# Bias of the edge list written by ScalarE, upper halves copied by Pool, edge stages in a new order

## The reference, cut to what matters

```python
hi = x @ W1[:H];  hj = x @ W1[H:]
h = relu(hi[:, :, None, :] + hj[:, None, :, :] + b1)   # one vector for each pair i, j
y = layernorm(h @ W2 + b2) * gamma + beta              # over the features
out = einsum('bij,bijh->bih', adj, y)                  # sum over the edges of node i
x = layernorm(x + out)
```

## Time and profile before

| what | value |
|---|---|
| three runs | 448.45, 449.18, 449.66 us |
| the profiled execution: its own time | 449.61 us |
| its span in the trace | 447.9 us |
| PE busy | 429.5 us (96%), 3391 instructions |
| DVE busy | 422.7 us (94%), 1555 |
| ACT busy | 393.8 us (88%), 1001 |
| Pool busy | 353.6 us (79%), 651 |

### The profile page before, as it was taken

How to read it: one execution, slowest core, us unless ns; L and a number is a source line. 1 busy time by engine, 2 the same in 40 slices (tenths; PEclk the granted TensorE clock), 3 DMA queues, 4 the chain that set the end, 5 groups by cost and what they waited for, 6 DMA issues and landing times. The chain is left out here.

```text
span 447.9 us, 14059 instructions
## 1 busy us (share of the span) xinstructions
PE 429.5 (96%) x3391; PEld 403.8 (90%) x3391; DVE 422.7 (94%) x1555; ACT 393.8 (88%) x1001; POOL 353.6 (79%) x651
## 2 busy tenths in 40 slices
PE   7599989999999999999999999999999999999993
PEld 3599989999999999898999999999999999999992
DVE  6999999999999999998999999999999999999976
ACT  2378979999999899979899999999999999999994
POOL 3569979999999899953776878787878787878772
PEclk9989999999999999999999999999999999999998
DMA  6134334445444743232422223222323232323111
GB/s 225 43 86 124 101 127 159 154 157 159 155 157 152 240 162 120 80 129 78 136 89 73 88 66 92 66 92 64 94 64 94 64 94 63 95 65 97 59 37 50
DMA packets 50939, 47.60 MB, mean 106 GB/s; under 512 B 5584, under 2 KB 42576, under 8 KB 50896
## 3 DMA queue, kind: packets, MB, share of 16 engines
q1 hardware_dynamic: 49760, 46.45, 33.7%
q10 hardware_dynamic: 1136, 0.66, 0.5%
HBM read 28.22 MB, written 18.87 MB: 105 GB/s over the span
## 5 line engine op out<-in xcount | busy, mean ns | idle before, releaser
L1621 PE MATMUL bank<-w2c,hE 128*128 128x128 f32 x512 | 68.3, 277 | 0.4 <-ACT bank L928 0.4
L1621 PEld LDWEIGHTS bank<-w2c,hE 128*128 128x128 f32 x512 | 63.5, 192 | 2.6 <-issue 0.7
L1289 DVE TENSOR_TENSOR ym<-bank,wE 128x512 f32<-128x512 f32 x64 | 43.4, 684 | 4.3 <-POOL wE L775 3.3
L1264 DVE TENSOR_REDUCE ssum<-sqE 128x4 f32<-128x512 f32 x63 | 42.7, 678 | 3.0 <-ACT sqE L945 2.7
L1122 DVE BATCH_NORM_STATS2 stats<-t 128x6 f32<-128x128 f32 x192 | 44.5, 273 | 1.0 <-issue 1.0
L945 ACT ACTIVATE sqE<-bank 128x512 f32<-128x512 f32 x63 | 38.0, 603 | 8.0 <-PE bank L1621 8.0
L915 ACT ACTIVATE hE<-bank,front 128x512 f32<-128x512 f32 x64 | 43.5, 680 | 1.5 <-PE bank L1601 1.5
L742 POOL TENSOR_TENSOR half<-ym 128x512 f32<-128x512 f32 x31 | 39.6, 1276 | 5.7 <-DVE ym L1289 2.1
L775 POOL TENSOR_TENSOR wE<-erstd,fits 128x12 f32<-128x12 f32 x31 | 6.6, 213 | 44.8 <-DVE erstd L1278 44.8
L726 POOL TENSOR_TENSOR gHl<-gH,gHu 128x512 fp32r<-128x512 f32 x32 | 40.8, 1276 | 1.2 <-ACT gHu L899 1.2
L928 ACT ACTIVATE bank<-b2c 128x512 f32<-128x512 f32 x62 | 37.4, 604 | 0.5 <-DVE ym L1289 0.4
(11 more groups left out here) (192 smaller groups left out, 1643.6 us busy)
## 6 DMA issues: line engine op xcount, KB each, us to landing
hh_scratch<-hh SPq DMA_DIRECT2D x32, 256.0 KB, 2.2
gH<-hh_scratch SPq DMA_DIRECT2D x32, 256.0 KB, 2.7
A<-adj_groups SPq DMA_DIRECT2D x32, 128.0 KB, 2.1
res_scratch<-res SPq DMA_DIRECT2D x32, 128.0 KB, 2.0
gRES<-res_scratch SPq DMA_DIRECT2D x32, 128.0 KB, 2.0
AT<-adjT_groups SPq DMA_DIRECT2D x31, 128.0 KB, 2.2
out<-y SPq DMA_DIRECT2D x30, 128.0 KB, 1.8
X<-x_groups SPq DMA_DIRECT2D x29, 128.0 KB, 2.2
```

Of the source, the lines that this page charges most:

```text
L1264: nc.vector.tensor_reduce(ssum[q][:, g * ELL:(g + 1) * ELL], sqE[g][:, :, :], AX.X, ALU.add).then_inc(b[f"ssE{g}_ready"], 1)
L1289: nc.vector.tensor_tensor(ym[q][:, g, :, :], YE_ps[g], spread_last(wE[q][:, g * ELL:(g + 1) * ELL]), ALU.mult).then_inc(b[f"ymE{g}_ready"], 1)
L1621: last = nc.tensor.matmul(ps[:, i, :], hidden[:, i * P:(i + 1) * P], w2c[:, :], start=False, stop=i == tiles - 1, skip_group_check=seeded)
```

## The change

Three edits and a new table.

1. `split_upper` goes from ScalarE. Pool's stage `hs` (`add_ends`) gets a `tensor_copy` of `gH` to `gHu` behind its addition, and waits for `HC_psum` of two units before as well.
2. ScalarE gets a stage `sdc` (`seed_csr`), which writes `b2c` into the bank for C once `yn` of the unit before has read it. PE's `mc` then waits for it and leaves out the bias product, except for unit 0.
3. SyncE's reload of `gH` is placed after `spl` alone, no longer after the later of `spl` and `hs`.
4. `T3` and `FIRST` have new numbers: the order of the edge stages on every engine, and their depth in slots, is made anew. The dense part's table is the same.

```diff
-        T3 = {"idx": 18.98, "rows": 29.95, "V": 33.91, "cols": 36.46, "g0": 34.64, "g1": 38.22, "gc": 38.09, "m0": 38.25, "m1": 38.57, "mc": 38.29,
-              "sc": 49.97, "spu": 17.7, "kS": 20.33, "kST": 26.68, "r0": 26.25, "r1": 27.55, "rc": 27.48, "sd0": 26.7, "sd1": 28.48, "s0": 28.66,
-              "s1": 30.86, "sqc": 29.86, "std": 31.27, "fstd": 47.6, "app": 55.95, "beg": 24.16, "T": 17.45, "Qp": 18.39, "T2": 28, "d0": 35.08,
-              "d1": 35.73, "dc": 35.41, "rec": 36.53, "x0": 40.69, "x1": 41.31, "yn": 41.92, "tot": 45.95, "st": 51.14, "ag": 51.41, "frec": 55.35,
-              "spl": 23.72, "hs": 25.25, "a1": 40.1, "a2": 42.41, "gm": 44.38, "rs": 45.6, "w": 35.72, "om": 52.88, "sh": 53.85}
+        T3 = {"idx": 9.51, "rows": 24.09, "V": 26.21, "cols": 29.26, "g0": 27.84, "g1": 29.68, "gc": 29.66, "m0": 32.08, "m1": 33.17, "mc": 32.86,
+              "sc": 42.66, "kS": 21.82, "kST": 25.93, "r0": 25.02, "r1": 28.16, "rc": 26.75, "sd0": 26.72, "sd1": 28.35, "sdc": 28.01, "s0": 28.7,
+              "s1": 30.21, "sqc": 29.08, "std": 33.26, "fstd": 47.06, "app": 56.31, "beg": 21.73, "T": 13.92, "Qp": 14.03, "T2": 25.57, "d0": 32.93,
+              "d1": 33.63, "dc": 33.42, "rec": 34.59, "x0": 37.13, "x1": 38.4, "yn": 37.59, "tot": 43.78, "st": 46.89, "ag": 47.17, "frec": 55.58,
+              "spl": 21.49, "hs": 20.41, "a1": 38.16, "a2": 41.2, "gm": 45.06, "rs": 46.11, "w": 34.67, "om": 47.92, "sh": 55.32}
...
-            edge_stages = [(("idx", 0.5), next_ot), (("spl", "hs", 1.5), next_h), (("rs", 0.8), next_res), (("app", 1), store)]
+            edge_stages = [(("idx", 0.5), next_ot), (("spl", 1.5), next_h), (("rs", 0.8), next_res), (("app", 1), store)]
...
                 wait_past(pool, b["HE1_psum"], count(2))
+                wait_past(pool, b["HC_psum"], count(2))
                 nc.gpsimd.tensor_tensor(hs[q][:, :, :], gH[q][:, :, 0:P], gH[q][:, :, P:2 * P], ALU.add).then_inc(b["hs_ready"], 1)
+                nc.gpsimd.tensor_copy(gHu[q][:, :, :], gH[q][:, :, :]).then_inc(b["split_up"], 1)
...
-            def split_upper(q, u, count):
-
-                act.wait_ge(gh_loaded[q], (u - q) * 8 + 16)
-                wait_past(act, b["HE1_psum"], count(2))
-                wait_past(act, b["HC_psum"], count(2))
-                nc.scalar.activation(gHu[q][:, :, :], gH[q][:, :, :], ACT.Copy).then_inc(b["split_up"], 1)
...
+            def seed_csr(q, u, count):
+                if isinstance(u, int) and u == 0:
+                    return
+                act.wait_ge(b["yC_ready"], count(1))
+                nc.scalar.activation(YC_ps, b2c[:, :].unsqueeze(1).to_broadcast([P, GROUP * CSR, P]), ACT.Copy).then_inc(b["seedC_done"], 1)
...
                 pe.wait_ge(b["hC_ready"], count())
-                wait_past(pe, b["yC_ready"], count(1))
-                project(YC_ps, hC, GROUP * CSR, "YC_psum")
+                seeded = not (isinstance(u, int) and u == 0)
+                if seeded:
+                    pe.wait_ge(b["seedC_done"], count(1))
+                project(YC_ps, hC, GROUP * CSR, "YC_psum", seeded)
```

More of the change, by code:

```diff
@@ L305, in gnn_stack @@
                   "esd_ready", "erstd_ready", "wE_ready", "ymE0_ready", "ymE1_ready", "yC_ready", "O_psum", "half_done", "accE_ready",
-                  "tot_ready", "gout_done", "tout_ready", "ostats_done", "omv_ready", "omean_ready", "ostd_ready", "orstd_done", "oshift_ready", "out_ready", "seedE0_done", "seedE1_done"]
+                  "tot_ready", "gout_done", "tout_ready", "ostats_done", "omv_ready", "omean_ready", "ostd_ready", "orstd_done", "oshift_ready", "out_ready", "seedE0_done", "seedE1_done", "seedC_done"]
         b = {n: sem("u_" + n) for n in names3}
@@ L364, in wait_past @@
                 engine.wait_ge(semaphore, n)
-        T3 = {"idx": 18.98, "rows": 29.95, "V": 33.91, "cols": 36.46, "g0": 34.64, "g1": 38.22, "gc": 38.09, "m0": 38.25, "m1": 38.57, "mc": 38.29,
[4 rows of a table removed]
+        T3 = {"idx": 9.51, "rows": 24.09, "V": 26.21, "cols": 29.26, "g0": 27.84, "g1": 29.68, "gc": 29.66, "m0": 32.08, "m1": 33.17, "mc": 32.86,
[4 rows of a table added]
         AGES = 4
         START3, EARLY, CATCH = 216.0, 5.0, 25.0
-        FIRST = {("Qp", 0): 219.13, ("Qp", 1): 221.26, ("Qp", 2): 230.17, ("Qp", 3): 240.76, ("Qp", 4): 250.69, ("Qp", 5): 261.11, ("Qp", 6): 305.61,
[7 rows of a table removed]
[L383 to L386, removed]
[4 rows of a table removed]
-                 ("frec", 3): 354.98, ("frec", 4): 377.23, ("frec", 5): 433.5, ("frec", 6): 479.84, ("frec", 7): 597.74, ("fstd", 0): 255.59,
-                 ("fstd", 1): 272.03, ("fstd", 2): 304, ("fstd", 3): 307.1, ("fstd", 4): 329.45, ("fstd", 5): 360.71, ("fstd", 6): 387.64,
[6 rows of a table removed]
[L399 to L402, removed]
[8 rows of a table removed]
-                 ("rec", 0): 230.93, ("rec", 1): 243.38, ("rec", 2): 253.14, ("rec", 3): 266.15, ("rec", 4): 286.69, ("rec", 5): 371.3,
-                 ("rec", 6): 380.43, ("rec", 7): 395.56, ("rows", 0): 220.19, ("rows", 1): 225.18, ("rows", 2): 231.18, ("rows", 3): 252.04,
-                 ("rows", 4): 273.75, ("rows", 5): 312.4, ("rows", 6): 322.8, ("rows", 7): 347.8, ("rs", 0): 239.21, ("rs", 1): 252.36,
[8 rows of a table removed]
-                 ("sh", 7): 368.47, ("spl", 0): 212.77, ("spl", 1): 218.79, ("spl", 2): 225.48, ("spl", 3): 235.56, ("spl", 4): 245.46,
-                 ("spl", 5): 259.39, ("spl", 6): 312.86, ("spl", 7): 374, ("spu", 0): 183.55, ("spu", 1): 217.3, ("spu", 2): 226.04,
-                 ("spu", 3): 232.29, ("spu", 4): 244.95, ("spu", 5): 254.16, ("spu", 6): 270.1, ("spu", 7): 284.7, ("sqc", 0): 228.99,
-                 ("sqc", 1): 236.21, ("sqc", 2): 245.83, ("sqc", 3): 259.45, ("sqc", 4): 276.27, ("sqc", 5): 277.67, ("sqc", 6): 292.79,
-                 ("sqc", 7): 376.85, ("st", 0): 249.46, ("st", 1): 262.52, ("st", 2): 275.92, ("st", 3): 336.82, ("st", 4): 372.9, ("st", 5): 374.49,
-                 ("st", 6): 400.55, ("st", 7): 412.66, ("std", 0): 231.68, ("std", 1): 239.35, ("std", 2): 251.61, ("std", 3): 264.53,
-                 ("std", 4): 314.04, ("std", 5): 322.9, ("std", 6): 327.82, ("std", 7): 334.05, ("tot", 0): 245.11, ("tot", 1): 254.06,
-                 ("tot", 2): 265.45, ("tot", 3): 271.56, ("tot", 4): 320.85, ("tot", 5): 338.09, ("tot", 6): 360.32, ("tot", 7): 453.47,
[5 rows of a table removed]
@@ new lines, in gnn_stack @@
+        FIRST = {("Qp", 0): 220.16, ("Qp", 1): 222.34, ("Qp", 2): 230.26, ("Qp", 3): 239.31, ("Qp", 4): 247.89, ("Qp", 5): 270.34, ("Qp", 6): 280.17,
[7 rows of a table added]
+                 ("app", 0): 261.82, ("app", 1): 285.19, ("app", 2): 325.24, ("app", 3): 325.42, ("app", 4): 371.4, ("app", 5): 382.81,
+                 ("app", 6): 397.12, ("app", 7): 414.99, ("beg", 0): 219.04, ("beg", 1): 220.58, ("beg", 2): 227.96, ("beg", 3): 242.53,
+                 ("beg", 4): 253.27, ("beg", 5): 256.8, ("beg", 6): 304.62, ("beg", 7): 431.25, ("cols", 0): 222, ("cols", 1): 229.76,
+                 ("cols", 2): 236.32, ("cols", 3): 253.77, ("cols", 4): 272.02, ("cols", 5): 298.9, ("cols", 6): 336.38, ("cols", 7): 339.34,
[4 rows of a table added]
+                 ("frec", 3): 328.53, ("frec", 4): 373.48, ("frec", 5): 375.37, ("frec", 6): 376.29, ("frec", 7): 384.36, ("fstd", 0): 256.87,
+                 ("fstd", 1): 278.32, ("fstd", 2): 282.64, ("fstd", 3): 315.8, ("fstd", 4): 348.95, ("fstd", 5): 374.03, ("fstd", 6): 383.01,
[6 rows of a table added]
+                 ("idx", 0): 203.32, ("idx", 1): 220.65, ("idx", 2): 229.03, ("idx", 3): 230.69, ("idx", 4): 242.32, ("idx", 5): 250.27,
+                 ("idx", 6): 271.96, ("idx", 7): 291.1, ("kS", 0): 220.3, ("kS", 1): 227.38, ("kS", 2): 230.48, ("kS", 3): 247.14, ("kS", 4): 252.69,
+                 ("kS", 5): 278.06, ("kS", 6): 290.92, ("kS", 7): 310.25, ("kST", 0): 224.07, ("kST", 1): 230.44, ("kST", 2): 243.77,
+                 ("kST", 3): 250.94, ("kST", 4): 270.12, ("kST", 5): 301.52, ("kST", 6): 308.51, ("kST", 7): 328.62, ("m0", 0): 218.19,
[8 rows of a table added]
+                 ("rec", 0): 230.91, ("rec", 1): 238.4, ("rec", 2): 250.89, ("rec", 3): 271.4, ("rec", 4): 325.86, ("rec", 5): 348.09,
+                 ("rec", 6): 394.41, ("rec", 7): 399.68, ("rows", 0): 218.58, ("rows", 1): 224.44, ("rows", 2): 231.84, ("rows", 3): 245.63,
+                 ("rows", 4): 255.11, ("rows", 5): 290.73, ("rows", 6): 297.63, ("rows", 7): 305.57, ("rs", 0): 244.02, ("rs", 1): 258.05,
[7 rows of a table added]
+                 ("sdc", 0): 232.92, ("sdc", 1): 233.54, ("sdc", 2): 239.14, ("sdc", 3): 254.24, ("sdc", 4): 266.16, ("sdc", 5): 314.09,
+                 ("sdc", 6): 319.35, ("sdc", 7): 381.5, ("sh", 0): 259.17, ("sh", 1): 304.76, ("sh", 2): 338.59, ("sh", 3): 352.68,
+                 ("sh", 4): 396.51, ("sh", 5): 417.74, ("sh", 6): 425.86, ("sh", 7): 436.09, ("spl", 0): 212.26, ("spl", 1): 225.74,
```

(10 more changed lines are left out.)

## The result

Four runs of the changed kernel give a median of 466.38 us (464.31 to 467.7), four of the kernel before 449.06 (448.45 to 449.66): 1.038 times as long (95% interval 1.033 to 1.043). That is 17.3 us more where 6.2 were predicted.

What follows compares the result with a forecast made beforehand. DVE's loop with a round trip over Pool was taken as the bound; the new slot, 0.73 + (2.13 + 0.57) + 4.31 = 7.74 us against 7.50, adds 6.2 over 26 slots to 449.18, giving 455.4 us, range 449 to 466.

Steps and rivals of the forecast that it cites:

- What bounds the kernel: Edge slots: DVE's own work plus one round trip over Pool sets the pace, 2.36 + 4.40 + 0.73 = 7.49 us.
- PE's bias product: Edge units on PE: dropping it frees 0.21 us in 31 of 32 units, counted as nothing since PE is outside DVE's loop.
- The new wait of `st` for `rs`: DVE's `st` must wait for Pool's `rs` of the same slot, behind `hs` and the copy: 0.34 us idle a slot.
- The price of the copy: Pool's new copy to `gHu`: 0.62 us, 0.57 after overlap; bounds for the latter 0.47 and 1.23.
- 0.24 a slot: New edge slot 7.74 us against 7.50; over 26 slots 6.2 us more.
- From the start of `st` to `rec` DVE needs 4.31: DVE's second stretch of the slot: 4.40 less 0.17 for the closed hole, plus 0.08 for `frec` in the open.
- The passage "0, with 2 us to either side": Slots with new orders in the passage: no change counted, 2 us either way, from 0.24 a slot for eight slots.
- `beg` counted as unchanged: DVE after `x0`: the stretch with `beg` kept at 2.36 us, after which DVE is free for `st`.
- PE's case: Rival, chance 0.13: PE's queue sets the slot, so 31 x 0.21 = 6.5 us go, giving 442.7 us.
- ACT's path: Rival, chance 0.16: `st` is not late and ACT's path of 7.51 to 7.61 us sets the slot; 449.4 to 452.0 us.
- The two-input price: Rival, chance 0.07: Pool's copy costs as much as a two-input operation, 1.23 us; +0.90 a slot, 472.6 us.

Runs made afterwards that it cites:

- e5_copy_twice: The changed kernel with a second, unused copy on Pool ahead of the real one; 481.59 us, ratio 1.070.
- e1_turn_moved: The changed kernel with `frec` ahead of `st`, so DVE's loop border lies between those two, otherwise the same order; 461.47 us, ratio 1.028.
- f3_passage: e1_turn_moved with three moments of `FIRST` changed, so that `ag` and the root of unit 1 come earlier; 459.15 us, ratio 1.022.
- e2_rs_first: The changed kernel with Pool's `rs` right behind `gm`, ahead of `hs` and the copy; 470.81 us, ratio 1.047.
- e4_copy_on_act: The changed kernel with the copy to `gHu` back on ScalarE, behind `std`; 469.98 us, ratio 1.047.
- f5_before_hole: The kernel before with only `T` moved between `st` and `ag` on DVE; 449.05 us, ratio 0.999.

## Where the prediction was right, and which step failed

- **What bounds the kernel**: right. In both kernels the sum of DVE's loop gives the slot: after, `x0` to `st` 2.78, `st` to `rec` 4.29 (309.80 to 314.09), `rec` to `x0` 0.65, together 7.72 against 7.73 measured; in the other slot 2.78, 4.89 and 0.83, together 8.50.
- **PE's bias product counted at nothing**: PE waits for DVE now. That it saves nothing by itself was not run alone, nor was the seed on ScalarE.
- **The new wait of `st` for `rs`**: right in place, and shown by e5_copy_twice. It was forecast as an idle time of 0.34 and shows as at most 0.1, because the stretched `beg` fills it. The price of the copy, 0.62, is right where nothing shares Pool's time (0.60 to 0.61) and 0.09 low in this kernel; one length alone doesn't show that it is made up of 0.21 and 0.83 ns a column. The 769 ns that the Trainium skill (GPSIMD Engine Reference, § 3.1 Elementwise) has for 512 elements in a tight loop is too long for this copy in either place.
- **0.24 a slot**: measured 0.31, or 0.29 where the turn is out of the way (e1_turn_moved). The 0.07 lie in `x0` to `st`, 2.78 for 2.70: the copy beside `beg`. Over 21 slots that is 6.5 us for 5.0; the written-out slots gave 1.1 for the 1.2 of the same step.
- **"From the start of `st` to `rec` DVE needs 4.31"**: this is the step that failed most, a term put at nothing. It holds in one slot (4.29); in the other it is 4.89, since the border of the hardware loop was moved between `d0` and `dc`. The prediction read the order of the stages from the table and left out where the turn stands in it; before, the turn costs nothing that shows. Ten times 0.60 are 6.0 us.
- **The passage "0, with 2 us to either side"**: the second step that failed; it was 4.5. `frec` waiting for the late root of unit 1 is 1.41 of it, and f3_passage shows that the order sets its length (2.79 to 1.36); the entry into the loop is 1.17. The other 1.9, in units 1 to 3, wasn't taken apart. (ScalarE loses six copies there and not five, by the table; neither number was priced.)
- **`beg` counted as unchanged**: the prediction gave the new Pool work a price on Pool and none on DVE. It doesn't add to the sum as long as `st` waits anyway, but it takes away every simple remedy (e2_rs_first, e4_copy_on_act).
- **The rivals**: no run gave the time of PE's case or ACT's path. ACT now waits 10.9 us for DVE, so its path doesn't bind. The two-input price falls with the copy's 0.60 to 0.71.

Together: 6.5 + 6.0 + 4.5 + 1.1 = 18.1 us of span, all of it located. Of these, 6.5 and 1.1 answer to the 6.2 that was forecast; the 6.0 of the turn and the 4.5 of the passage were forecast at nothing. The turn is settled by experiments in both directions, the passage only in part, and no run gave the 6.5 back.

## What to carry to other kernels

When an order in a hardware loop is made anew, look where the turn of the loop falls in each engine's queue, and price it on the engine that sets the pace. Price an instruction that moves to Pool twice: on Pool, and on those VectorE instructions beside it that it holds, as `beg` here and not the sums. When a second loop lies close under the one that binds, removing a wait gives the time to the next (in f5_before_hole less than 0.05 of 0.17 a slot was left), so a remedy must be summed round all of them.
